# A routed feed-forward on one core: weights in 4 KB pieces, transposes that read with a stride, and a reordered hand-over

## What is computed

```python
logits = x @ router_w
scores = sigmoid(logits)                       # 32 experts in 8 groups
...                                            # best 4 groups, then best 8 experts
tkw = scores of the 8 experts, normed to sum 1, times 2.5
gate = ragged_dot(xs, w_gate, group_sizes)     # xs: tokens sorted by expert
up   = ragged_dot(xs, w_up, group_sizes)
down = ragged_dot(silu(gate) * up, w_down, group_sizes)
routed = (down[unsort].reshape(T, K, H) * tkw[..., None]).sum(axis=1)
shared = silu(x @ sw_gate) * (x @ sw_up) @ sw_down
return routed + shared
```

## Time and profile before

| | |
|---|---|
| median of 3 runs | 1054.2 us |
| the profiled execution | 1052.7 us, of which the span of its instructions 1050.9 us |
| mean granted TensorE clock | 0.935 of full speed |
| first block | 0 to 285.4 us |
| hand-over | 285.4 to 326.5 us |
| tile loop on TensorE | 326.5 to 1038.3 us |
| instructions on TensorE (matmul) / VectorE / ScalarE | 4604 / 1321 / 994 |

### The profile page before, as it was taken

One profiled execution on the slowest core, in us unless ns is written; L12 is line 12 of the kernel. 1 busy time (PEld: TensorE's weight loads), 2 busy tenths in 40 slices (PEclk: granted clock), 3 DMA queues, 4 the chain that ended last, 5 costly groups with the idle time before them and its releaser, 6 DMA issues.

```text
span 1050.9 us, 21209 instructions
## 1 busy us (share of the span) xinstructions
PE 915.5 (87%) x4604; PEld 493.5 (47%) x4605; DVE 577.8 (55%) x1321; ACT 490.8 (47%) x994; POOL 430.3 (41%) x348
## 2 busy tenths in 40 slices
PE   4259688888777999999999999999999999999994
PEld 1144354535343555555545544545545554545542
DVE  5958798889775334446453454444454445454331
ACT  5376472743032443446454454444455454463331
POOL 2011001110023555554665554545555564655653
PEclk8569888797888999999999999999999999999998
DMA  5211020111227687778888778778778788877654
GB/s 160 89 41 52 16 84 35 41 43 41 71 94 264 139 186 177 165 174 211 185 187 177 172 174 202 143 204 183 167 201 190 219 183 219 183 168 135 126 105 74
DMA packets 90271, 149.27 MB, mean 142 GB/s; under 512 B 9649, under 2 KB 46769, under 8 KB 90225
## 3 DMA queue, kind: packets, MB, share of 16 engines
q0 software_dynamic: 33120, 80.64, 39.3%
q1 hardware_dynamic: 57104, 68.13, 19.6%
HBM read 101.55 MB, written 47.20 MB: 142 GB/s over the span
## 4 chain that ended last, share of the span: by engine, by line
PE 54%; issue 6%; DVE 4%; ACT 3%; DVEq 2%; ACTq 2%; DMA 0%; POOL 0%; SPq 0%; POOLq 0%
PE bank L258 46%; PE bank L1487 5%; PE bank L1478 3%; ACT gu L240 2%; DVEq L1170 2%; ACTq L1170 1%; DVE gu L247 1%; DVE hid L1401 1%; PE bank L1459 0%; DVE mark_p L400 0%; ACT xgT L1257 0%; DVE mark_q L407 0%; DMA stage_dn<-in_L_ffn_w_down_dram 0%; DVEq L247 0%; ACTq L240 0%
## 5 line engine op out<-in xcount | busy, mean ns | idle before, releaser
L258 PE MATMUL bank<-gu,xgT 128*128 x1764 | 407.6, 381 | 10.3 <-issue 7.0
L1213 POOL DMA_INDIRECT out_dram<-y,ids_i x145 | 235.5, 1624 | 276.0 <-DMA out_dram<-y,ids_i 143.1
L258 PEld LDWEIGHTS bank<-gu,xgT 128*128 128x128 f16 x1764 | 172.7, 98 | 190.6 <-issue 18.2
L258 PE MATMUL bank<-dn,hT 128*128 x870 | 211.7, 379 | 15.3 <-issue 15.3
L1393 DVE TENSOR_TENSOR xgT<-bank,xgT 128x512 f16<-128x512 f32 x148 | 101.8, 688 | 166.2 <-ACT xgT L1257 166.2
L1201 POOL DMA_INDIRECT xg<-xrows,ids_i x153 | 158.7, 1037 | 64.0 <-issue 39.3
L1401 DVE SCALAR_TENSOR_TENSOR hid<-bank,xg,silu 128x256 f32<-128x256 f32 x147 | 70.8, 482 | 169.8 <-ACT silu L1263 163.9
L1263 ACT ACTIVATE silu<-bank 128x256 f32<-128x256 f32 x147 | 55.7, 379 | 206.7 <-PE bank L258 204.9
L1282 ACT ACTIVATE y<-bank 128x512 f32<-128x512 f32 x145 | 86.9, 599 | 125.4 <-PE bank L258 125.4
L258 PEld LDWEIGHTS bank<-dn,hT 128*128 128x128 f16 x870 | 84.8, 98 | 89.7 <-issue 22.2
L247 DVE SCALAR_TENSOR_TENSOR gu<-stage_gu,gu (+1 forms) x64 | 75.5, 1221 | 56.0 <-ACT gu L240 56.0
(11 more groups left out here) (217 smaller groups left out, 770.6 us busy)
## 6 DMA issues: line engine op xcount, KB each, us to landing
stage_gu<-in_L_ffn_w_gate_dram SPq DMA_DIRECT2D x32, 512.0 KB
stage_gu<-in_L_ffn_w_up_dram SPq DMA_DIRECT2D x32, 512.0 KB
stage_dn<-in_L_ffn_w_down_dram SPq DMA_DIRECT2D x32, 512.0 KB
x_sb<-in_x_dram SPq DMA_DIRECT2D x4, 1024.0 KB, 6.6
xrows<-adj SPq DMA_DIRECT2D x4, 1024.0 KB, 4.2
out_dram<-acc SPq DMA_DIRECT2D x4, 1024.0 KB, 4.7
xg<-xrows,ids_i POOLq DMA_INDIRECT x153, 4.4
out_dram<-y,ids_i POOLq DMA_INDIRECT x145, 5.1
```

The costliest lines, as they stand in the source:

```text
L258: last = nc.tensor.matmul(out_ap, stationary(a, c), moving(w, c), start=(c == 0 and (a, w) == parts[0]), stop=(c == chunks - 1 and (a, w) ...
L1213: g_.indirect_dma_start(out, bass.IndirectOffsetOnAxis(ap=ids_i[:, t:t + 1], axis=0), y[:, t % YS, :], None, compute_op=ALU.add).then_inc( ...
```

## The change

Five things are changed.

1. `load` lays four consecutive rows (down: two) of a matrix in one partition, so that every piece is 4 KB. The staging tile and the halves in which it is converted change with it: a half is now all of gate or all of up. To match, a transpose of `xg` takes every fourth column (`c:H:KC`, a step of 16 bytes) and a transpose of `hid` every second (`c:I:IC`, a step of 8 bytes). The matmuls on the shared expert keep their layout.
2. `tab` and `onehot` are float16.
3. In the tile loop all `info_of` of a step stand at its start, on TensorE, ScalarE and VectorE.
4. The end of the first block: `s_add(p, 3)` of the last sequence moves into the middle of `routing`; `rank_tokens`, `count_columns`, `turn_found` and `find_keys` move to the start of the second block; SyncE's waits for shares and zeros go.
5. The hand-over: another order on all three engines, one `convert_high` earlier and one conversion later, `s_down(b, 0)` ahead of `list_rows`, and the last `s_down` and `s_add` behind the transposes of the first two tiles. `DB` gives these products other banks.

```diff
-        DB = (7, 5, 6, 7)
+        DB = ((7, 5, 6, 7),) * (B - 1) + ((6, 7, 5, 1),)
...
-                return gu16[:, n % WS, part, 2 * piece:2 * piece + 2, :].rearrange("p k n -> p (k n)")
+                return gu16[:, n % WS, part, :, piece * I:(piece + 1) * I]
...
-            sp.dma_start(gu[:, :, 0, :], g.rearrange("(k p) i -> p k i", p=P)).then_inc(S["weights_loaded"], 16)
-            sp.dma_start(gu[:, :, 1, :], u.rearrange("(k p) i -> p k i", p=P)).then_inc(S["weights_loaded"], 16)
-            sp.dma_start(dn[:, :, :], d.rearrange("(k p) h -> p k h", p=P)).then_inc(S["weights_loaded"], 16)
+            sp.dma_start(gu[:, 0, :, :], g.rearrange("(p k) i -> p k i", p=P)).then_inc(S["weights_loaded"], 16)
+            sp.dma_start(gu[:, 1, :, :], u.rearrange("(p k) i -> p k i", p=P)).then_inc(S["weights_loaded"], 16)
+            sp.dma_start(dn[:, :, :], d.rearrange("(p k) h -> p k h", p=P)).then_inc(S["weights_loaded"], 16)
...
                 sp.wait_ge(S["rows_stored"], 16 * (B + 1))
-                sp.wait_ge(S["shares_stored"], 16 * B)
-                sp.wait_ge(S["zeroed"], 16)
...
                         sum_marks(pe, p)
-                        s_gate_up(pe, b, 1, (0,))
-                        rank_tokens(pe, b)
-                        count_columns()
-                        s_gate_up(pe, b, 1, (1,))
-                        turn_found(pe, p)
+                        s_gate_up(pe, b, 1)
...
                     if b + 1 < B:
                         search_step(b + 1, 2)
+                    else:
+                        s_add(dve, b - 1, RT - 1)
...
                 split_rows(0, 0)
                 split_rows(1, 1)
+                for e in range(1, AHEAD):
+                    convert_high(act, SH + e)
                 gates(0, 0)
...
                     s = i % 2
+                    fresh, e = info_of(act, 1, t), info_of(act, 0, t)
                     split_rows(t + 2, s)
-                    next_weights(t)
+                    next_weights(fresh, e)
                     gates(t + 1, 1 - s)
...
+                find_keys(dve, ch, b)
+                s_product(dve, b, 1)
                 count_tiles()
                 mark(dve, b, 0)
                 mark(dve, b, 1)
-                s_product(dve, b, 1)
+                s_product(dve, b, 2)
+                find_slots()
                 mark(dve, b, 2)
+                s_product(dve, b, 3)
                 mark(dve, b, 3)
-                s_product(dve, b, 2)
                 round_uses()
-                find_slots()
                 list_tiles()
-                s_product(dve, b, 3)
+                s_add(dve, b, 0)
                 list_rows()
                 convert_low(dve, SH)
-                for i in range(RT):
+                for i in range(1, RT - 1):
                     s_add(dve, b, i)
-                for e in range(1, AHEAD):
-                    convert_low(dve, SH + e)
...
                 b = B - 1
+                rank_tokens(pe, b)
+                count_columns()
+                turn_found(pe, b - 1)
                 s_gate_up(pe, b, 2)
-                s_gate_up(pe, b, 3, (0,))
+                s_gate_up(pe, b, 3)
                 sum_starts()
+                list_tiles()
                 sum_marks(pe, b)
-                s_gate_up(pe, b, 3, (1,))
-                list_tiles()
                 turn_found(pe, b)
+                s_down(pe, b, 0)
                 list_rows()
-                for i in range(RT):
+                for i in range(1, RT - 1):
                     s_down(pe, b, i)
                 pe.wait_ge(S["tables_ready"], 1)
-                pe.wait_ge(S["added"], TT)
...
-                        t = nc.tensor.transpose(bank[HT[s]][:, c * P:(c + 1) * P], hid[:, s, c * P:(c + 1) * P], ident[:, :])
+                        t = nc.tensor.transpose(bank[HT[s]][:, c * P:(c + 1) * P], hid[:, s, c:I:IC], ident[:, :])
...
-                        last = nc.tensor.transpose(bank[XB[s]][:, c * P:(c + 1) * P], xg[:, x, c * P:(c + 1) * P], ident[:, :])
+                        last = nc.tensor.transpose(bank[XB[s]][:, c * P:(c + 1) * P], xg[:, x, c:H:KC], ident[:, :])
...
+                pe.wait_ge(S["added"], TT - 3)
                 rows_T(0, 0, 0)
+                pe.wait_ge(S["added"], TT - 2)
                 rows_T(1, 1, 1)
-                gate_up_of(0, 0)
+                s_down(pe, b, RT - 1)
+                gate_up_of(0, 0, info_of(pe, 0, 0))
+                pe.wait_ge(S["added"], TT)
...
                     s = i % 2
+                    e, before_e = info_of(pe, 0, t + 1), info_of(pe, 0, t - 1)
                     rows_T(t + 2, s, (i + 4) % XG)
-                    gate_up_of(t + 1, 1 - s)
+                    gate_up_of(t + 1, 1 - s, e)
                     hidden_T(t, s)
-                    down_of(t - 1, 1 - s)
+                    down_of(t - 1, 1 - s, before_e)
```

More of the change, by code:

```diff
@@ L642, in logits @@
                     t.then_inc(S["logits_ready"], 1)
-                def count_columns():
-                    pe.wait_ge(S["found_ready"], B - 1)
-                    for b in range(B):
-                        nc.tensor.matmul(bank[INFO][:, b:b + 1], earlier[:, b * RT:(b + 1) * RT, :].rearrange("p g e -> p (g e)"),
-                                         ones[:, 0:1], start=True, stop=True)
-                    nc.tensor.matmul(bank[INFO][0:E, B:B + 1], earlier[:, TT, :], ones[:, 0:1],
-                                     start=True, stop=True).then_inc(S["columns_ready"], 1)
                 context_T(0)
@@ L1106, in _ @@
                     routing(b)
-                    if p >= 0:
+                    if p >= 0 and more:
                         s_add(dve, p, 3)
@@ L1123, in _ @@
                         s_product(dve, b, 0)
-                        find_keys(dve, ch, b)
         phase.close()
@@ L1263, in gates, with next_weights @@
                     a_.activation(silu[:, s, 0:I], bank[GU[s]][:, 0:I], ACT.Silu, scale=1.0 / W_SCALE).then_inc(S["tile_silu"], 1)
-                def next_weights(t):
-                    with act.If(info_of(act, 1, t) > 0):
-                        convert_high(act, info_of(act, 0, t) + (SH + AHEAD))
+                def next_weights(fresh, e):
+                    with act.If(fresh > 0):
+                        convert_high(act, e + (SH + AHEAD))
                 def hidden(t, s):
@@ L1394, in split_rows, with gates @@
                                     ALU.subtract).then_inc(S["rows_low"], 1)
-                def gates(t, s, x):
-                    share = xg[:, x, bass.ds(info_of(dve, 0, t) + H, 1)]
+                def gates(t, s, x, e):
+                    share = xg[:, x, bass.ds(e + H, 1)]
                     dve.wait_ge(S["tile_silu"], t + 1)
@@ L1402, in gates, with next_weights @@
                                            ALU.mult, ALU.mult).then_inc(S["tile_hid"], 1)
-                def next_weights(t):
-                    with dve.If(info_of(dve, 1, t) > 0):
-                        convert_low(dve, info_of(dve, 0, t) + (SH + AHEAD))
+                def next_weights(fresh, e):
+                    with dve.If(fresh > 0):
+                        convert_low(dve, e + (SH + AHEAD))
                 def hidden(t, s):
@@ L1414, in _ @@
                 split_rows(1, 1)
-                gates(0, 0, 0)
+                s_add(dve, b, RT - 1)
+                for e in range(1, AHEAD):
+                    convert_low(dve, SH + e)
+                gates(0, 0, 0, info_of(dve, 0, 0))
                 def step(t, x):
                     s = x % 2
+                    fresh, e, next_e = info_of(dve, 1, t), info_of(dve, 0, t), info_of(dve, 0, t + 1)
                     split_rows(t + 2, s)
-                    next_weights(t)
-                    gates(t + 1, 1 - s, (x + 1) % XG)
+                    next_weights(fresh, e)
+                    gates(t + 1, 1 - s, (x + 1) % XG, next_e)
                     hidden(t, s)
@@ L1437, in _, with count_columns @@
             def _(pe):
+                def count_columns():
+                    pe.wait_ge(S["found_ready"], B - 1)
+                    for b in range(B):
+                        nc.tensor.matmul(bank[INFO][:, b:b + 1], earlier[:, b * RT:(b + 1) * RT, :].rearrange("p g e -> p (g e)"),
+                                         ones[:, 0:1], start=True, stop=True)
+                    nc.tensor.matmul(bank[INFO][0:E, B:B + 1], earlier[:, TT, :], ones[:, 0:1],
+                                     start=True, stop=True).then_inc(S["columns_ready"], 1)
                 def sum_starts():
@@ L1506, in hidden_T, with down_of @@
                     transposes(s).then_inc(S["tile_hidT"], 1)
-                def down_of(t, s):
-                    w_slot = (info_of(pe, 0, t) + SH) % WS
+                def down_of(t, s, e):
+                    w_slot = (e + SH) % WS
                     pe.wait_ge(S["tile_hlo"], t + 1)
```

36 lines of the change are left out of this document (17 added, 19 removed).

## The result

The kernel after took 1046.19 us, the median of 5 runs (1043.55 to 1047.02), against 1055.27 us (1052.93 to 1055.89) for the kernel before on the same chip. The ratio is 0.9911, 95% interval 0.9891 to 0.9930: faster by 0.9%, about 9 us, where 1014 us had been forecast. The sign was right, the size was not: the time is near that of rival B (1043).

The account below looks back on a forecast made before the run. TensorE's own work was taken to bound the loop, with 43.7 us of stalls. 1052.7 - 30 (register reads) - 11 (hand-over) = 1011.7, about 1013 against the median; 1014 us was forecast, range 1005 to 1067.

Parts of the forecast that it names:

- rival B: Tile loop: the moved reads only shift the gap ahead of `rows_T`; only the hand-over gains, 1043 us; chance 0.10.
- What bounds the kernel: Tile loop: TensorE's own work, 4.54 us a plain tile, plus 43.7 us of stalls, mostly around a new expert.
- Register reads at the start of a step: Tile loop: reads covered by queued down matmuls, conversions up to 1.03 us earlier; gain 30 us, bounds 10 to 40.
- R: Tile loop, theory of the follow-up experiments: a register read holds its queue for 0.68 us and its place decides.
- End of the first block: Before the loop: earlier sum, TensorE's wait 0.9 us, 24 matmuls at full clock; `find_keys` earlier, gain so far 3.4 us.
- Hand-over: Before the loop: row numbers near 307.9, first tile's products near 317.5, 9 us earlier; gain 11 us, bounds 4 to 15.
- 4 KB pieces: Weight loading: fewer packets, but TensorE's plain tile doesn't see it; 0 taken, bounds 0 to a gain of 5 us.
- The stride: Transposes of `xg` and `hid` in the loop: strided reads taken to cost 0, with 54 us kept as far end.
- Rival C: Tile loop: strided weight loads of the transposes cost 54 us while the gains stay; 1067 us, 1050 to 1075; chance 0.36.

Follow-up runs that it names:

- the last kernel: The kernel after with reads among queued work, last `s_down` ahead of the second tile's transposes, 1 and 2 KB weight pieces, transposes in order: 1013.72 us, ratio 0.9622.

## Why the prediction was right or wrong

**What bounds the kernel: right.** Of 43.7 us of stalls about 28 can be had, and they stood at the register reads: the last kernel has 16.1 left.

**Register reads at the start of a step: wrong, and this is the miss.** The gain was put at 30 us with bounds of 10 to 40; it was 0. Two sentences failed. The first is that 1.29 us of down matmuls cover "two reads of at most 0.5 us each". The 0.47 us of the earlier trace rows is not the length of a read but what was left of it behind 0.22 us of transposes: a read takes 0.68, two take 1.36, and the subtraction 0.90 - 0.22 could have been made from the rows. And the reads don't start with the down matmuls. Behind a late `hid` they start some 0.9 us after the transposes, so that of 0.22 + 1.29 us about 0.6 are left to cover 1.36. That is the gap at an edge of an expert. Placed under 2.59 us of work, the same two reads cost next to nothing: R holds.

The second is "On ScalarE the reads lie under the `result` copy, so a conversion starts up to 1.03 us earlier". A queue in order reaches the reads only when the copy is released, by TensorE's down products. In the rows above two reads take 1.90 us from there (412.61 to 414.51, one of the loads being a slow one), the copy hides 0.60 of them, and the cast that used to stand ahead of the reads, and cover another 0.58, now stands behind. By the median the conversion starts 0.2 us earlier, in the rows shown 0.28 later. The `hid` waits do fall, 5.5 to 2.1 us, but nothing comes of it.

**B's mechanism was named and under-rated.** "The gap appears ahead of `rows_T`" is what happened, at 1043 against 1046.19. It had a chance of 0.10, because the argument against it was the cover of 1.29 us, held against a read that had been sized too short and counted from the wrong moment.

**End of the first block: right.** TensorE's wait for the sum is 0.88 us (0.9 forecast), the 24 matmuls take 5.34 us at the full clock (5.3). Counted from the earlier 24, `find_keys` stands at 13.69 us after and at 16.86 before: 3.2 us earlier, 3.4 forecast.

**Hand-over: right in kind, too large.** `s_down(b, 0)` took 4.27 us (5.1 forecast), `list_rows` 0.74 (1.1). The row numbers are ready at 305.47, or 307.2 with the 1.8 us of scatter; 307.9 was forecast. The clock was up on the first tile's products, 2.75 us, as hoped. Wrong is the rest of the path: from the row numbers to those products 9.6 us were forecast and 14.3 passed. The second tile's gather is issued behind the first and its rows are there only at 314.06, 8.6 us after the row numbers, where the sum had 6.5 (9.6 less 0.5 and 2.6): "a second gather behind it" had no more than 0.2 us in it, and the two issues are 2.2 us apart (305.77 and 307.98); and `s_down` behind that wait ran at the low clock, 4.94 us instead of 2.6. So the hand-over gave 7.5 us by the profiles, 11 forecast (4 to 15).

**4 KB pieces: right.** 0 forecast, 0 to 5 as bounds; 1.8 us by the medians of one set, 3.0 to 4.7 by single profiles. The packets of the queue halved and its share of the DMA time stayed.

**The stride: right at the near end, by a wrong estimate of the load.** 0 was taken, 54 kept; the runs give 4 to 6 us. The load was thought unchanged; it grew by about 60 ns, and a transpose by 0.01 us. The limit that was set for it, 0.11 us, was the wrong one: the loads take 140 ns in order and 196 to 208 with a step, both more than the 0.11 us in which transposes follow each other, and they overlap. That a load consists of passes of 50 ns is shown by no run, and the earlier trace rows has 335 ns as the median beside the 190 that it was taken from. So the term was right by luck as much as by reasoning. The rule of the Trainium skill ("SBUF — State Buffer", Specifications) has it that lines of 16 bytes must be hit twice for full bandwidth, so that a step of 8 bytes would be free; here a step of 8 (`hid`, 196 ns) is as slow as one of 16 (`xg`, 208). The trace does not agree with that part. Rival C, with 0.36, was far off, although one of its signs came, loads over 200 ns: ScalarE's copy was no guide to what a strided load costs.

## What to carry to other kernels

A read of a table from SBUF into a register is an instruction of its queue, and in these traces nothing behind it starts before it has ended: size it by how late the next instruction is, with what covered it added back, and count its cover from the moment at which the queue reaches it. Place it right behind the longest run of work that is queued without a wait, here twelve matmuls, and not at the start of a step behind an instruction that may be waiting; that alone was worth 22 us, while collecting the reads at the start was worth nothing. One read in place of two left no gap there either, except where three had been put in a row. When a gap has no semaphore of its own, look for the one ahead of it in the same queue.

## What was not expected of the hardware

- A register read from SBUF occupied TensorE's queue for 0.68 us (0.61 by the median of 304), of which the load is 0.30 (295 to 957 ns) and the register operations 0.15. The Trainium skill gives a floor of some 600 ns for `tensor_load` ("DMA: Bandwidth & Descriptors", Latency and other measured facts); the load's own record is half of that here, the whole read is near it.
- A float32 weight load of 128 columns took 140 ns in order and 196 to 208 ns with a step of 8 or 16 bytes. As a part of a transpose it cost 0.01 us.
- 28432 packets took the same share of the DMA engines' time as 57104 with the same 68.13 MB.
- What stays open: what the 16 us of stalls of the last kernel are in detail (some 3 are gaps in the last eight tiles), and whether 4 KB pieces without a stride, which would need another way to match the columns, would keep their 1.8 us there. Neither was tried.
